# Attention scores in 32-row tiles of the array, two heads at once, two query tiles per step, with the attention turn laid out anew

## What is computed

```
h = table[tok] + lora_A[tok] @ lora_B
x = layernorm(h)
cq, ckv = layernorm(x @ W_dq) * g + b, layernorm(x @ W_dkv) * g' + b'
Q, K, V = cq @ W_uq, ckv @ W_uk, ckv @ W_uv          # 16 heads of 32
o = softmax(mask(Q K^T / sqrt(32))) V                # per head, 128 x 128, causal
h = h + o @ W_o.T
h = h + ffn(layernorm(h))
```

## Time and profile before

| | before |
|---|---|
| median of 3 runs | 2663.51 us |
| profiled execution, its own time | 2662.18 us |
| its span (first to last instruction) | 2660.4 us |
| TensorE busy | 2530.0 us, 95% |
| ScalarE, VectorE, GpSimd busy | 1837.2, 1695.1, 1129.0 us |
| mean granted TensorE clock | 0.985 |

### The profile page before, as it was taken

How to read it: one execution, slowest core, us unless ns; L and a number is a source line. 1 busy time by engine, 2 the same in 40 slices (tenths; PEclk the granted TensorE clock), 3 DMA queues, 4 the chain that set the end, 5 groups by cost and what they waited for, 6 DMA issues and landing times.

```text
span 2660.4 us, 49271 instructions
## 1 busy us (share of the span) xinstructions
PE 2530.0 (95%) x13120; PEld 1890.3 (71%) x13120; DVE 1695.1 (64%) x3742; ACT 1837.2 (69%) x4597; POOL 1129.0 (42%) x1275
## 2 busy tenths in 40 slices
PE   3899999999999999689999999999999999999999
PEld 2666666666666665467888888888888888888887
DVE  5666666666666665366765765676576567657655
ACT  1666677777777777376866876786686678668666
POOL 4333343334334432123644544454454445446445
PEclk8999999999999999789999999999999999999999
DMA  3222222222121211241222122132222213212221
GB/s 112 56 65 64 64 64 64 64 64 64 64 64 64 64 48 37 92 143 63 98 88 84 51 96 86 40 108 86 69 69 95 86 41 107 83 57 86 91 72 60
DMA packets 99750, 197.23 MB, mean 74 GB/s; under 512 B 10928, under 2 KB 10928, under 8 KB 99568
## 3 DMA queue, kind: packets, MB, share of 16 engines
q1 hardware_dynamic: 94576, 179.29, 20.4%
q0 software_dynamic: 5120, 17.31, 2.5%
HBM read 145.66 MB, written 50.86 MB: 74 GB/s over the span
## 4 chain that ended last, share of the span: by engine, by line
issue 29%; POOL 24%; PE 2%; DVE 1%; ACT 1%; POOLq 1%; DMA 0%; SPq 0%; DVEq 0%; ACTq 0%
POOL t_lo L1181 23%; POOL sh_lo L1181 1%; POOLq L1179 1%; DVE ps_u L1550 0%; DVE f_lo L1575 0%; DMA x<-h 0%; ACT x L1344 0%; DVE t L1557 0%; ACT t_hi L1399 0%; PE ps_g L1196 0%; PE ps_g L1198 0%; PE ps_u L1198 0%; PE ps_u L1196 0%; PE ps_u L1197 0%; PE ps_g L1197 0%
## 5 line engine op out<-in xcount | busy, mean ns | idle before, releaser
L1181 POOL TENSOR_TENSOR t_lo<-t,t_hi 128x512 fp32r<-128x512 f32 x512 | 665.1, 1299 | 423.5 <-ACT t_hi L1399 423.4
L395 POOL TENSOR_TENSOR probs<-probs,inv 128x512 f32<-128x512 f32 x256 | 265.1, 1041 | 577.1 <-DVE inv L803 577.1
L622 ACT ACTIVATE probs<-ps_s,nmax 128x128 f32<-128x128 f32 x1024 | 362.4, 371 | 153.1 <-DVE nmax L798 149.9
L1550 DVE TENSOR_TENSOR ps_u<-ps_u,square 128x512 f32<-128x512 f32 x512 | 357.0, 697 | 159.0 <-ACT square L1386 154.3
L1399 ACT ACTIVATE t_hi<-t 128x512 fp32r<-128x512 f32 x512 | 320.5, 626 | 119.9 <-PE ps_y L1198 69.0
L1557 DVE TENSOR_TENSOR t<-ps_u,w_all 128x512 f32<-128x512 f32 x512 | 354.0, 691 | 60.7 <-DMA w_all<-w_rows 20.7
L1382 ACT ACTIVATE square<-ps_g 128x512 f32<-128x512 f32 x544 | 319.8, 588 | 91.6 <-PE ps_g L1198 89.5
L1386 ACT ACTIVATE square<-square 128x512 f32<-128x512 f32 x544 | 344.2, 633 | 17.3
L513 PE MATMUL ps_s<-k_diag,qT 128*128 128x512 f32 x512 | 261.4, 592 | 0.0
L798 DVE TENSOR_REDUCE nmax<-ps_s 128x4 f32<-128x512 f32 x256 | 174.3, 681 | 126.5 <-PE ps_s L513 124.1
L1196 PE MATMUL ps_y<-t_hi,f_hi 128*128 128x512 f32 x512 | 209.9, 410 | 13.2 <-POOL t_lo L1181 13.0
(11 more groups left out here) (196 smaller groups left out, 5502.9 us busy)
## 6 DMA issues: line engine op xcount, KB each, us to landing
w_all<-w_rows SPq DMA_DIRECT2D x256, 256.0 KB, 3.1
h<-h SPq DMA_DIRECT2D x64, 256.0 KB, 2.7
res<-h SPq DMA_DIRECT2D x64, 256.0 KB, 2.8
h<-res SPq DMA_DIRECT2D x64, 256.0 KB, 2.0
x<-h SPq DMA_DIRECT2D x16, 1024.0 KB, 5.7
fres<-h SPq DMA_DIRECT2D x16, 1024.0 KB, 7.3
out<-fres SPq DMA_DIRECT2D x64, 256.0 KB, 2.7
fres<-in_w_ffn SPq DMA_DIRECT2D x14, 512.0 KB, 3.6
```

The lines of the kernel that those rows point to most:

```text
L395: pool.tensor_tensor(probs[:, s % 4, :, :], probs[:, s % 4, :, :], inv[:, s % 4, :].rearrange("p (h o) -> p h o", o=1).to_broadcast([P, HP ...
L622: e = act.activation(probs[:, s % 4, j, :], ps_s[:, s % 2, j, :], ACT.Exp, bias=nmax[:, s % 4, j:j + 1], accum_out=total[:, s % 4, j:j + 1])
L1181: pool.tensor_tensor(lo, t[:, t_slot(j), :], hi.bitcast(F32), ALU.subtract).then_inc(t_lo_done, 1)
L1550: dve.tensor_tensor(dst, product, square[:, j % 2, :], ALU.mult).then_inc(t1_done, 1)
```

## The change

Scores are now made for two slots at a time, in the even steps, and without `k_diag`. The keys stand as they come (`kT`), and a head's 32 rows are multiplied alone, in a tile of 32 rows of the array. With x = 0, 1 and y = 0, 1, head 2x + y goes to bank x. First come the 4 matmuls of y = 0 (two slots i, two banks x), then one bf16 mask matmul for each bank, then, after a wait of TensorE on its own semaphore `rows_free`, the 4 of y = 1. `ps_s` has now two pairs of banks; to make room, `ps_t` and `ps_o` have one bank each instead of two. `row_max` reads two banks (1024 elements for each partition) in one instruction; the exponentials stay 4 for each slot.

With it the turn is laid out anew: T_LAG 3 instead of 2, PV_LAGS (6, 5, 6, 5) instead of 4, so that the products with V of two slots stand together in even steps; ScalarE copies `pT` ahead of the step's exponentials; rings of 8 for `probs`, 4 for `pT`, 2 for `oT`; other steps for nearly all parts; `k` is copied whole by ScalarE, `v` 2 and 3 and `q` 3 by VectorE; and the loop's body holds two turns.

```diff
-INV_LAG, NORM_LAG, T_LAG, PV_LAG = 1, 1, 2, 4
+INV_LAG, NORM_LAG = 1, 2
+T_LAG, C_LAG = 3, 3
+RING = 8
+PV_LAGS = (6, 5, 6, 5)
+TURN_FIRST, COPY_FIRST = False, True
...
-          3: (("v", 1), ("h", 3)), 5: (("v", 2),), 6: (("out", 0),), 9: (("out", 3),), 12: (("wd", 0),),
+          9: (("out", 1),), 14: (("wd", 0), ("k", 0)), 15: (("out", 3),)}
...
-STATS_AT, NORM_AT, C_NORM_AT, SPLIT_AT = (3, 5), 8, 4, 14
+STATS_AT, NORM_AT, C_NORM_AT, SPLIT_AT = (3, 5), 7, 4, 13
...
-        ps_s = pb("ps_s", [P, 2, HPC, P], F32)
-        ps_t = pb("ps_t", [P, 2, HPC * P], F32)
-        ps_o = pb("ps_o", [P, 2, TOK], F32)
+        ps_s = pb("ps_s", [P, 2, ROW_TILES, ROW_HEADS, 2, P], F32)
+        ps_t = pb("ps_t", [P, HPC * P], F32)
+        ps_o = pb("ps_o", [P, TOK], F32)
...
-                at_least(pe, exp_done, SLOTS * n + s - 1)
-                pe.matmul(ps_s[:, s % 2, :, :], ident_b[:, :], mask[:, :, :], start=True, stop=False,
-                          skip_group_check=True)
-                pe.matmul(ps_s[:, s % 2, :, :], qT[:, m, t * P:(t + 1) * P], k_diag[:, m, t, :, :],
-                          start=False, stop=True, skip_group_check=True).then_inc(scores_full, 1)
+                at_least(pe, exp_done, SLOTS * n + s - 2)
+                banks = ps_s[:, (s // 2) % 2]
+                for y in range(ROW_HEADS):
+                    if y == 1:
+                        pe.wait_ge(rows_free, SLOTS * n + s + 2)
+                    for i in range(2):
+                        for x in range(ROW_TILES):
+                            head = ROW_HEADS * x + y
+                            rows = slice(head * DH, (head + 1) * DH)
+                            mm = pe.matmul(banks[:, x, y, i, :], qT[rows, m, (t + i) * P:(t + i + 1) * P],
+                                           kT[rows, m, (t + i) * P:(t + i + 1) * P],
+                                           start=(y == 0 and i == 0), stop=(y > 0), skip_group_check=True)
+                            if y == 0 and i == 1:
+                                mm.then_inc(rows_free, 1)
+                    if y == 0:
+                        for x in range(ROW_TILES):
+                            pe.matmul(banks[:, x, :, :, :], ident_b[:, :], mask[:, :, :], start=False, stop=False,
+                                      skip_group_check=True)
+                mm.then_inc(scores_full, 2)
...
-                at_least(pe, pT_done, SLOTS * n + s - 1)
+                at_least(pe, pT_done, SLOTS * n + s)
...
-                for j in range(K_ON_DVE[i], HPC):
-                    op = act.activation(k_diag[j * DH:(j + 1) * DH, i, :, j, :],
-                                        bank_of(n, "k", i)[j * DH:(j + 1) * DH, :].rearrange("p (t k) -> p t k", t=TILES),
-                                        ACT.Copy)
-                was_read(op, n, "k", i, 1)
+                was_read(act.activation(kT[:, i, :], bank_of(n, "k", i), ACT.Copy), n, "k", i)
...
-                dve.wait_ge(scores_full, SLOTS * g + s + 1)
-                dve.tensor_reduce(nmax[:, s % 4, :], ps_s[:, s % 2, :, :], AX.X, ALU.max,
-                                  negate=True).then_inc(max_done, 1)
+                dve.wait_ge(scores_full, SLOTS * g + s + 2)
+                b = (s // 2) % 2
+                dve.tensor_reduce(nmax[:, b, :, :, :].rearrange("p x y i -> p (x y i)"),
+                                  ps_s[:, b, :, :, :, :].rearrange("p x y i k -> p (x y i) k"), AX.X, ALU.max,
+                                  negate=True).then_inc(max_done, 2)
```

More of the change, by code:

```diff
@@ L130, in is_turn @@
+ACT_BEHIND = ()
+DVE_BEHIND = (("h", 0), ("out", 2), ("xt", 1), ("xt", 2))
+PAIRS = (GROUPS - 4) // 2
 def is_turn(n, which):
@@ L270, in attention_phase @@
         scores_full = sem("scores_full")
+        rows_free = sem("rows_free")
         max_done = sem("max_done")
@@ L331, in _, with turn @@
                          lora_lo[RANK:2 * RANK, :].bitcast(F32)).then_inc(lora_placed, 16)
-            def turn(n):
+            def turn(n, side):
+                if has_part(n, "h", 0):
+                    for t in range(TILES):
+                        bank, before = place(n, "h", t)
+                        wait_alone(sp, work_free[bank], DRAINS * (before + 1), sp_passed)
+                        sp.dma_start(h2[bass.ds((n + 2) * TOK + t * P, P), :],
+                                     h[:, t, :]).then_inc(res_kept[t], 16)
                 for i in range(TILES + 1):
@@ L413, in turn @@
                         newton_of(2 * NEWTON_OPS * (n + 1) + NEWTON_OPS, 2 * TILES)
-            gather(0)
+            pick(0)
+            for t in range(TILES):
+                gather(0, t)
             for n in (-2, -1, 0):
-                turn(n)
-            with pool.Fori(1, GROUPS - 3) as n:
-                turn(n)
-            for n in range(GROUPS - 3, GROUPS + 1):
-                turn(n)
+                turn(n, n % 2)
+            with pool.Fori(0, PAIRS) as k:
+                turn(2 * k + 1, 1)
+                turn(2 * k + 2, 0)
+            for n in range(2 * PAIRS + 1, GROUPS + 1):
+                turn(n, n % 2)
         @block.tensor
@@ L662, in turn @@
                     if step in O_HI_AT and has_slot(n, 0 if O_HI_AT[step] < 2 else -1):
-                        o_hi(n, O_HI_AT[step])
+                        o_hi(n, side, O_HI_AT[step])
+                    if COPY_FIRST and has_slot(n, step - C_LAG):
+                        pT_copy(n, step - C_LAG)
                     if has_slot(n, step):
@@ L781, in k_copy @@
             def k_copy(n, i):
[L782 to L788 removed]
+                was_read(dve.tensor_copy(kT[:, i, :], bank_of(n, "k", i)), n, "k", i)
             def add_out(n, t):
@@ L841, in turn @@
                     read_work(n, midway_of(step, DVE_AHEAD, True))
-                    if has_slot(n, step):
+                    if step in O_LO_AT and has_slot(n, 0 if O_LO_AT[step] < 2 else -1):
+                        o_lo(n, side, O_LO_AT[step])
+                    if step % 2 == 0 and has_slot(n, step):
                         row_max(n, step)
@@ L897, in _ @@
             for n in (-2, -1, 0):
-                turn(n)
-            with dve.Fori(1, GROUPS - 3) as n:
-                turn(n)
-            for n in range(GROUPS - 3, GROUPS + 1):
-                turn(n)
+                turn(n, n % 2)
+            with dve.Fori(0, PAIRS) as k:
+                turn(2 * k + 1, 1)
+                turn(2 * k + 2, 0)
+            for n in range(2 * PAIRS + 1, GROUPS + 1):
+                turn(n, n % 2)
 LAT, HID, EXPERTS, TOP = 128, 256, 16, 8
```

217 lines of the change are left out of this document (105 added, 112 removed).

## The result

The changed kernel takes 2622.1 us (median of 4 runs, 2619.9 to 2628.0) against 2663.4 us of before, measured beside it (2659.5 to 2664.3): ratio 0.985, with a 95% interval of 0.983 to 0.987. The prediction was 2584; half of the forecast change came, 41 us instead of 80. The profiled execution took 2623.7 us.

What follows compares the result with a forecast made beforehand. TensorE, busy 95% of the span, was taken as the bound; -3.35 us in 16 turns and -1.95 in 14 made 81 us, less 1 for the drain: 2584 us against 2663.5, range 2566 to 2640 (8 in 10).

Steps and rivals of the forecast that it cites:

- Scores: TensorE's score matmuls: a half of 0.68 us, bounded below by 0.64, 16 a turn, so -2.8 us a turn.
- Rival B: Score halves: passes pair up imperfectly, five rounds instead of four, half 0.80 us, +31, 2615 us; chance 0.13.
- rival C: Score halves: a tile's next weights cannot load while its pass streams, half 0.96 us, +72, 2656 us; chance 0.06.
- rival D: Score halves: row tiles do not overlap at all, half 1.07 to 1.15 us, 2684 to 2704 us; chance 0.11.
- the prediction's estimate for two: Score halves, from the skill page's packing figure: if two tiles lose the same share, a half 0.77 us, sum 2607.
- Masks, products with V, boundaries: TensorE's other work in a turn: masks +0.1 us, products with V -1.1, exits from and entries into small tiles +0.45.
- The cover of `rows_free` by the masks: TensorE between score halves: masks (0.53 us) hide the semaphore wait, costed at nothing; uncovered some 0.2 us a pair.
- The wait of the down projection: TensorE's wait for the low half of x goes, its pieces being turned two steps earlier: -1.95 us in 14 turns.
- Sum -3.35 us a turn: TensorE time of a turn: scores -2.8, masks +0.1, products with V -1.1, boundaries +0.45; for all 16 turns with scores.
- the drain of +1: End of the attention loop: longer lags lengthen the drain, 1 us of the gain taken back.
- E: Rival: with one `ps_t` bank, TensorE's transposes wait for ScalarE's copy, 1 to 3 us a turn, 2600 to 2632; chance 0.10.
- case A: Main case: half 0.64 to 0.75 us, other waits as they are, 2570 to 2605 us; chance 0.60.

Runs made afterwards that it cites:

- run 1: Changed kernel with TensorE's loop of six two-turn bodies written out, no branch back in the attention phase: 2576.9 us against 2631.1 of before, ratio 0.980.
- run 4: Kernel before with TensorE's 13 loop turns written out, nothing else: 2628.8 us against 2630.5 of before, ratio 0.9993.
- the third run of group 5: Changed kernel with TensorE written out, masks ahead of both score halves instead of between them: 2581.3 us, ratio 0.981 to before.
- Run 7: Kernel before with GpSimd's four gathers one each in steps 10 to 13: 2630.1 us against 2630.5 on one chip, 2630.3 against 2666.1 on another.
- the second run of group 5: Changed kernel with TensorE written out, each half's four score matmuls ordered bank by bank: 2575.8 us, ratio 0.978 to before.
- run 6: Both kernels unchanged on another chip: changed kernel 2623.6 us against 2631.7 of before, ratio 0.997; before again, for its profile, 2629.4 us.

## Why the prediction was half right

**Scores.** Right. The step put a half at 0.68 with a lower bound of 0.64; it measures 0.643, the entry of 0.21 and four rounds of a pass, 0.107. Weight loads do not stretch the round here. Rival B (0.80) and rival C (0.96) are out, and so is rival D, whose price of 1.07 to 1.15 was right for what it described: with the rows made equal, a half takes 1.083. The Trainium skill, "TensorE: Matmul & The Clock Gate", Part 3, lets weight loads overlap only where the row group differs; those eight passes on the same rows disagree, (1.083 - 0.21) / 8 = 0.109 each with their loads. The same part of the Trainium skill has a speed-up of 3.07 for four row tiles, from which the prediction's estimate for two was 0.77; the runs show no such loss for two.

**Masks, products with V, boundaries.** Right: 0.54 for 0.53, 0.57 for 0.58, transposes behind small tiles 0.59. The turns without a branch are 59.1 to 60.1 us where 59.8 was forecast, and the -3.35 us for each of 16 turns, -54 in all, are the -52 between runs 1 and 4. The cover of `rows_free` by the masks is shown in the third run of group 5: without it the two halves take 0.16 us more a pair at the least.

**The wait of the down projection.** The size was nearly right, by luck, since the reason was wrong. The step said that the wait goes because the pieces of x are turned two steps earlier. Run 7 has the old order and no wait. It came with TensorE's signals arriving late around four gathers in a row, on some chips, and it was worth more than the 1.95 us read: 65.1 against 62.6 us a turn, 32 us in all instead of 27. The change takes it away, along with the delays behind it. Where the chip doesn't have it, the same change is worth 32 us less.

**What was not in the sum: the branch.** This is the step that failed. "Sum -3.35 us a turn", "Turn 59.8" and the drain of +1 stand there, and for the doubled loop body, which the section on the change names, no term. Each way back takes 4 to 5 us instead of 0.2, TensorE stands still for 3.3 to 4.6 us around it, and the clock falls behind it: 47 us between the medians with and without the branches (2623.6 and 2576.9), 51 between their profiled executions. With 47 the prediction would have been 2631, and 5 less with the wait at its true size: 2626 against the 2622 measured. The profile of before had a trace of it, the branch of 0.2 us, and the number of TensorE's instructions in a turn could be counted from the earlier trace rows (3230 matmuls in eight turns and as many loads); what a longer body costs, no row of before could tell. The rivals looked for a new wait between engines (E); `ps_t` with one bank, which E named, cost nothing: TensorE's waits view of the changed kernel has no wait for `pT`.

**The range** of 2566 to 2640 contains 2622, but for the wrong reason: its upper half stood for imperfect pairing and a new wait, and case A alone (2570 to 2605) does not reach it. The feed-forward phase kept its length, as said.

**The other engines.** As forecast, none is near the turn's length: in the good turn ScalarE is busy 42.0 us (42.5 forecast), GpSimd 25.6 (25.6) and VectorE 40.5, just above the 34 to 40 forecast.

**Balance.** On the chips where before takes 2631: scores and layout -52 to -56 (run 1 against run 4, and the second run of group 5 against before), branches +47, together near the -8 of run 6. Where it takes 2663 to 2666: -32 to -36 more. The changed kernel with TensorE written out is the best version measured, 2576.9 us against 2631.1 on one chip, and 2575.5 against 2666.1 on another (with the gathers in a row); its gain over the changed kernel, 47 us, is larger than the 41 of the change.

## What to carry to other kernels

Before a loop body is made longer on the fullest engine, count its instructions, loads included, and look at what the branch takes now; if the longer body may no longer stay at hand, write the loop out or keep the body short, and give the branch a term of its own in the sum; here it was 2 us without and 9 to 11 with the half clock behind it. A wait that the trace ascribes to an order of work is that order's only if the signal between the two engines was prompt: compare the end of the releaser with the start of the waiter, and profile the kernel on a second chip. Two row tiles paid in full here when they were on different rows within a run of four matmuls, and what separates two runs of them on a semaphore should have real work under it.

## What the runs showed of the hardware

- A branch back of TensorE: 0.21 us with a body of 888 instructions, 4.1 to 5.0 with 1770, 2170 or 4330. TensorE stands still for 2 us around it with 1770 and for 3.3 to 4.6 with 2170, and still works for the first 2 to 2.6 us of it.
- A standstill of 3.3 to 4.6 us was followed five times out of five by 17.1 us at half clock in the changed kernel (in run 6 four times, and once by 13.7), and one of about 2 us in the old kernel by 3.4 us of it twice in five. With TensorE busy all along the clock fell for 3.4 us too, six times in the run with equal rows.
- Two row tiles of 32 rows, f32: eight passes of 128 columns in 0.643 us on two row groups (0.650 in the other order of the list), 1.083 on one.
- The same program, before, takes 2631 us on three chips and 2663 to 2666 in two other measurements, each to 0.3%; in the one trace of the slower kind, signals from TensorE to VectorE and ScalarE came up to 4.0 us late around four gathers issued in a row. With the gathers one a step the difference is gone.
